# An attention and expert kernel: ranking steps moved and rewritten, and other products before the first real one

## The reference, cut to what matters

```python
x = x + xattn(layernorm(x), ctx, Wq, Wk, Wv, Wo, bo)     # x (4, 256, 128), ctx (4, 1601, 96)
x = x + ffn(layernorm(x), ...)                            # 1024 tokens

def xattn(x, context, Wq, Wk, Wv, Wo, bo):                # 8 heads of 64
    q, k, v = heads(x @ Wq), heads(context @ Wk), heads(context @ Wv)
    attn = softmax(q @ k.T * 64 ** -0.5)
    return merge(attn @ v) @ Wo + bo

def ffn(flat, router_w, router_b, sw1, sb1, sw2, sb2, rw1, rb1, rw2, rb2):   # 8 experts
    probs = softmax(flat @ router_w + router_b)
    top, idx = top_k(probs, 2)
    weights = zeros_like(probs).at[rows, idx].add(top)    # not normalised again
    shared = gelu(flat @ sw1 + sb1) @ sw2 + sb2
    h1 = gelu(einsum('td,edh->teh', flat, rw1) + rb1)
    return shared + einsum('ted,te->td', einsum('teh,ehd->ted', h1, rw2) + rb2, weights)
```

## Time and profile before

| | |
|---|---|
| median of 3 runs | 435.71 us |
| profiled execution: time, span | 435.49 us, 433.7 us |
| TensorE, products, busy | 420.8 us, 97% of the span |
| VectorE, ScalarE, GpSimd busy | 278.3, 219.3, 257.8 us |
| chain that ended last, by engine | TensorE 83%, GpSimd 8%, VectorE 3%, ScalarE 2% |
| mean granted clock of TensorE | 0.992 of full speed |

### The profile page before, as it was taken

The page is one execution under the profiler, slowest core; times in us unless marked ns, Lnnn a source line. Parts: engine busy times, 40 slices in busy tenths (PEclk is TensorE's granted clock), DMA queues, the critical chain, the costliest instruction groups (busy, mean ns, idle before and its releaser), DMA issues.

```text
span 433.7 us, 7166 instructions
## 1 busy us (share of the span) xinstructions
PE 420.8 (97%) x2500; PEld 327.0 (75%) x2500; DVE 278.3 (64%) x553; ACT 219.3 (51%) x384; POOL 257.8 (59%) x176
## 2 busy tenths in 40 slices
PE   8999999999999999999999999999999999878997
PEld 6787777786877877777878786778686776756896
DVE  4785858785546858673458596743495865656553
ACT  3555353342763534336735353447244754883783
POOL 4628995868474849382757483917352900873981
PEclk9999999999999999999999999999999999997999
DMA  7400002000000020000000300000000032003200
GB/s 227 139 1 2 0 2 59 0 2 0 2 0 2 2 58 2 0 2 0 2 2 0 110 2 2 2 1 0 2 2 2 2 97 79 19 1 112 85 26 24
DMA packets 16329, 11.59 MB, mean 27 GB/s; under 512 B 9580, under 2 KB 13208, under 8 KB 16296
## 3 DMA queue, kind: packets, MB, share of 16 engines
q1 hardware_dynamic: 16296, 11.15, 9.5%
HBM read 10.55 MB, written 0.56 MB: 26 GB/s over the span
## 4 chain that ended last, share of the span: by engine, by line
PE 83%; POOL 8%; DVE 3%; ACT 2%; issue 1%; DMA 1%; SPq 1%; POOLq 0%; ACTq 0%
PE ps L1254 19%; PE ps L1238 10%; PE ps L1174 10%; PE ps L1239 10%; PE ps L1240 10%; PE ps L1086 7%; PE ps L1088 7%; PE ps L1087 7%; POOL work L559 4%; PE ps L1128 2%; PE ps L1186 1%; POOL g_lo L773 1%; DMA probs<-in_L_xattn_Wv_dram 1%; POOL w_lo L757 1%; POOL work L557 1%
## 5 line engine op out<-in xcount | busy, mean ns | idle before, releaser
L849 ACT ACTIVATE probs<-ps 128x512 f32<-128x512 f32 (+1 forms) x208 | 123.8, 598 | 134.8 <-PE ps L1240 127.8
L970 DVE TENSOR_REDUCE maxes<-ps 128x1 f32<-128x402 f32 x256 | 131.6, 567 | 55.4 <-PE ps L1174 55.3
L559 POOL TENSOR_TENSOR work<-work,probs 128x1024 f32<-128x1024 f32 x54 | 128.9, 2388 | 15.9 <-ACT probs L849 13.0
L1254 PE MATMUL ps<-probs,v_sb 128*64 128x256 f32 (+1 forms) x832 | 93.4, 381 | 0.0
L1254 PEld LDWEIGHTS ps<-probs,v_sb 128*64 128x64 f32 (+1 forms) x832 | 58.3, 137 | 33.9 <-ACT probs L849 3.7
L1238 PE MATMUL ps<-g_hi,ctxT_hi 97*128 97x512 f32 (+1 forms) x208 | 82.9, 399 | 0.0
L557 POOL TENSOR_TENSOR work<-probs 128x1024 f32<-128x1024 f32 x14 | 33.5, 2392 | 82.0 <-issue 61.6
L1239 PE MATMUL ps<-g_lo,ctxT_hi 96*128 96x512 f32 (+1 forms) x208 | 82.0, 394 | 0.0
L1240 PE MATMUL ps<-g_hi,ctxT_lo 96*128 96x512 f32 (+1 forms) x208 | 81.7, 393 | 0.0
L1174 PE MATMUL ps<-ctxT_hi,g_hi 96*128 96x402 f32 x256 | 72.6, 356 | 0.7 <-ACT ctxT_hi L788 0.4
L773 POOL TENSOR_TENSOR g_lo<-probs,g_hi 128x512 fp32r<-128x512 f32 x32 | 40.5, 1290 | 35.1 <-ACT g_hi L871 35.1
(11 more groups left out here) (147 smaller groups left out, 526.4 us busy)
## 6 DMA issues: line engine op xcount, KB each, us to landing
v_sb<-weight_rows SPq DMA_DIRECT2D x12, 256.0 KB, 4.0
raw<-in_ctx_T_dram SPq DMA_DIRECT2D x3, 600.4 KB, 4.5
work<-in_L_ffn_rw_dram SPq DMA_DIRECT2D x1, 1024.0 KB, 7.5
raw<-weight_rows SPq DMA_DIRECT2D x4, 256.0 KB, 3.6
g_hi<-neg_row SPq DMA_DIRECT2D x60, 0.5 KB, 2.0
raw<-in_ctx_T_dram SPq DMA_DIRECT2D x3, 150.8 KB, 2.8
x_sb<-in_x_dram SPq DMA_DIRECT2D x1, 384.0 KB, 5.6
early<-in_WqkT_dram SPq DMA_DIRECT2D x1, 336.0 KB, 5.1
```

What stands on the lines that cost most here:

```text
L559: ops.tensor_tensor(acc, acc, pr, ALU.add).then_inc(summed, 1)
L849: nc.scalar.activation(probs[0:rows, n % SLOTS, j, :], s_bank(chunk_no(*w))[0:rows, :], ACT.Exp, scale=SCALE).then_inc(probs_ready, 1)
L970: v.tensor_reduce(maxes[:, p % 2, i * T + t, blk:blk + 1], src[:, 0:BW], AX.X, ALU.max).then_inc(ring_taken, 1)
L1254: ins = mm(o_bank[DH * i:DH * (i + 1), :], v_sb[0:rows, c, h * DH:(h + 1) * DH], probs[0:rows, n % SLOTS, j, i * S:(i + 1) * S], start=(c ...
```

## The change

- **Last half's routing.** The transposes of the last batch's rows (`xt`), the router and the exponential each move one turn later. `rank` comes at the end of turn 6 and the transposes of the weights at the end of turn 7, behind the second layer's products of that turn.
- **Ranking rewritten.** The two best are found from the logits less their maximum, not from the probabilities: `mark_best` replaces the two largest by 1.0 and makes a mask of them (`is_gt` 0.5). In the last half it follows the logits at once, beside the exponential. Then exponential times mask, sum, reciprocal, and one product written into all four groups of columns. In the last half the exponential and its masked form stand in PSUM. The low part of the weights is now made after the transposes (one more VectorE step). The first half uses the same steps on VectorE, GpSimd has none of them any more, and the first half's logits also have their maximum subtracted (one exponential instead of four).
- **w1 in three parts**: experts 0 to 2 after pair 0, 3 and 4 after pair 2, together with the addition of `bo`, 5 to 8 after pair 3.
- **Start.** Instead of 13 fp32 products of 128 rows and 64 columns: 8 pairs of `float32r` products, each of 64 rows, 128 stationary and 256 moving columns, on rows 0 to 63 and 64 to 127, into banks 4 and 5. The memset of `ones_r` stands ahead of that of `ones`. The later `keep_awake` calls stay.
- **First casts.** ScalarE converts all four blocks of the first context before `Wv`, and GpSimd takes two low parts before `wv_lo`.

```diff
-WARM = 13
+WARM = 8
...
-              (n_units + 1, 3): [("rank",), ("best",)], (3, 6): [("ring", ("wrow",))]}
+              (n_units + 1, 3): [("rank",)], (3, 6): [("ring", ("wrow",))]}
...
-        main += [("w1", k) for k in range(2) if n == 2 * k] + followers(n, n_units)
+        main += [("w1", k) for k, at in enumerate((0, 2, 3)) if n == at] + followers(n, n_units)
...
-    amid = {0: [("sums", last_pair), ("quotient", last_pair + (0,)), ("quotient", last_pair + (1,))], 2: [("ring", ("y", b))], 4: [("ring", ("xt", b))],
-            5: [("ring", ("router", last)), ("exp", last)], 6: [("rank", last), ("best", last)], 7: [("ring", ("wrow", last))]}
-    behind = {2: [("roots", b)], 3: [("norm", b)]}
+    amid = {0: [("sums", last_pair), ("quotient", last_pair + (0,)), ("quotient", last_pair + (1,))], 2: [("ring", ("y", b))], 5: [("ring", ("xt", b))],
+            6: [("ring", ("router", last)), ("exp", last)]}
+    behind = {2: [("roots", b)], 3: [("norm", b)], 6: [("rank", last)], 7: [("ring", ("wrow", last))]}
...
-    W1_CUT = NE - PAIRS
+    W1_PARTS = (slice(0, PAIRS - 1), slice(PAIRS - 1, PAIRS + 1), slice(PAIRS + 1, NE))
...
+        ones_r = sb("ones_r", [P, S], F32R)
...
+        lexp_bank, chosen_bank = (ps[:, O_BANK, i * TH * E:(i + 1) * TH * E].rearrange("p (t e) -> p t e", e=E)
+                                  for i in range(2))
+        def routing(w):
+            return (lexp_bank, chosen_bank) if w == NHALF - 1 else (lexp[:], chosen[:])
...
+            own(g.memset(ones_r[:].bitcast(F32), 1.0))
             own(g.memset(ones[:], 1.0))
...
             low_part(0, 0)
+            low_part(0, 1)
             pool.wait_ge(s_wv, 16)
...
-                if kind == "scores" and w == (0, 3, NU - 1, 0):
-                    added(0, 3)
+                if kind == "w1" and w == 1:
+                    added(0, 2)
                     pool.wait_ge(xn_ready, B - 1)
                     pool.wait_ge(s_bo, 16)
                     g.tensor_tensor(x_sb[:], x_sb[:], bo_sb[:].unsqueeze(1).to_broadcast([P, NT, D]), ALU.add
...
+                    nc.scalar.activation(routing(w)[0], logit[:, :, 0:E], ACT.Exp).then_inc(lexp_ready, 1)
...
-                if p == 0 and b < 2:
-                    dve.wait_ge(w1_split, b + 1)
+                if (b, p) in ((0, 0), (0, 2), (1, 0)):
+                    dve.wait_ge(w1_split, ((0, 0), (0, 2), (1, 0)).index((b, p)) + 1)
...
+            def mark_best(w):
+                dve.wait_ge(logit_ready, w + 1)
+                for t in range(TH):
+                    ins = v.max(top8[:, t, :], logit[:, t, 0:E])
+                then_own(ins)
+                then_own(v.memset(top8[:, :, TOP:8], 1.0))
+                for t in range(TH):
+                    ins = v.match_replace(low[:, t, 0:E + 8 - TOP], top8[:, t, :], logit[:, t, 0:E + 8 - TOP], 1.0)
+                then_own(ins)
+                then_own(v.tensor_scalar(mask[:], low[:, :, 0:E], 0.5, None, ALU.is_gt))
...
+                        then_own(v.tensor_reduce(neg_lmax[:], lg, AX.X, ALU.max, negate=True))
+                        v.tensor_tensor(lg, lg, neg_lmax[:].unsqueeze(2).to_broadcast([P, TH, E]), ALU.add
                                         ).then_inc(logit_ready, 1)
+                        if b == NHALF - 1:
+                            mark_best(b)
...
-                        v.tensor_copy(wT[:, b * HALF:(b + 1) * HALF], src).then_inc(ring_taken, 1)
+                        cols = slice(b * HALF, (b + 1) * HALF)
+                        then_own(v.tensor_copy(wT[:, cols], src))
+                        v.tensor_tensor(wT[WLO:WLO + E, cols], src[WLO:WLO + E, :], wT[WLO:WLO + E, cols].bitcast(F32),
+                                        ALU.subtract).then_inc(ring_taken, 1)
                 elif kind == "rank":
+                    le, ch = routing(w)
+                    if w < NHALF - 1:
+                        mark_best(w)
                     dve.wait_ge(lexp_ready, w + 1)
+                    v.tensor_tensor(ch, le, mask[:], ALU.mult)
+                    then_own(v.tensor_reduce(lsum[:], le, AX.X, ALU.add))
                     then_own(v.reciprocal(rsum[:], lsum[:]))
...
+                    wr = wrow[:, w * TH:(w + 1) * TH, :].rearrange("p t (a r) -> p t a r", r=WLO)[:, :, :, 0:E]
+                    v.tensor_tensor(wr, ch.unsqueeze(2).to_broadcast([P, TH, P // WLO, E]),
+                                    rsum[:].unsqueeze(2).unsqueeze(3).to_broadcast([P, TH, P // WLO, E]), ALU.mult
+                                    ).then_inc(w_ready, 1)
...
-            keep_awake(WARM)
+            for _ in range(WARM):
+                for r in range(2):
+                    rows = slice(DH * r, DH * r + DH)
+                    mm(ps[:, 4 + r, 0:S], ones_r[rows, 0:P], ones_r[rows, :], start=True, stop=True)
+            pe.wait_ge(pool_done, 2)
```

More of the change, by code:

```diff
@@ L380, in build @@
         w_rows = sb("w_rows", [P, NHALF, HALF])
-        logit = sb("logit", [P, TH, E])
+        logit = sb("logit", [P, TH, E + 8])
+        mask = sb("mask", [P, TH, E])
         neg_lmax = sb("neg_lmax", [P, TH])
@@ L385, in build @@
         rsum = sb("rsum", [P, TH])
-        rprob = sb("rprob", [P, TH, E + 8])
+        chosen = sb("chosen", [P, TH, E])
         top8 = sb("top8", [P, TH, 8])
@@ L506, in twice @@
             return rows.rearrange("p t (a r) -> p t a r", r=W3)
-        def high_weights(rows):
-            return (twice(rows)[:, :, :, 0:E], w_hi[:].bitcast(F32).unsqueeze(2).to_broadcast([P, TH, P // W3, E]))
         def activations(n):
@@ L605, in _ @@
             load_ctx(1)
-            sp.wait_ge(pool_done, 4)
+            sp.wait_ge(pool_done, 5)
             sp.dma_start(b2_rows[0:E], rb2).then_inc(s_b2, 16)
@@ L697, in _ @@
             g.tensor_tensor(wv_lo[:], wv_sb, wv_hi[:].bitcast(F32), ALU.subtract).then_inc(w_split, 1)
-            for i in range(1, BLOCKS):
+            for i in range(2, BLOCKS):
                 low_part(0, i)
@@ L701, in _ @@
             pool.wait_ge(consts_ready, 2)
[L702 removed]
+            g.memset(logit[:], 1.0).then_inc(consts_ready, 1)
             pool.wait_ge(s_rw, 32)
@@ L752, in _ @@
                 if kind == "w1":
-                    es = (slice(0, W1_CUT), slice(W1_CUT, NE))[w]
+                    es = W1_PARTS[w]
                     pool.wait_ge(s_w1, 32)
-                    added(0, 2 * w)
+                    added(0, (0, 2, 3)[w])
                     then_own(g.tensor_copy(w1_hi[:, es], w1_sb[:, es]))
@@ L804, in _ @@
                 high_part(0, i)
-                if i == 1:
-                    act.wait_ge(s_wv, 16)
-                    nc.scalar.copy(wv_hi[:], wv_sb).then_inc(wv_hi_ready, 1)
+            act.wait_ge(s_wv, 16)
+            nc.scalar.copy(wv_hi[:], wv_sb).then_inc(wv_hi_ready, 1)
             for kind, w in steps:
@@ L995, in _ @@
                             dve.wait_ge(s_rw, 32)
-                        v.tensor_tensor(logit[:], src[:, 0:TH * E].rearrange("p (t e) -> p t e", e=E),
+                        lg = logit[:, :, 0:E]
+                        if b == 0:
+                            dve.wait_ge(consts_ready, 3)
+                            dve.wait_ge(s_rw, 32)
+                        v.tensor_tensor(lg, src[:, 0:TH * E].rearrange("p (t e) -> p t e", e=E),
                                         rb_sb[:].unsqueeze(1).to_broadcast([P, TH, E]), ALU.add).then_inc(ring_taken, 1)
                         dve.wait_ge(*taken(w))
[L999 to L1004, removed]
+                        then_own(v.tensor_reduce(neg_lmax[:], lg, AX.X, ALU.max, negate=True))
+                        v.tensor_tensor(lg, lg, neg_lmax[:].unsqueeze(2).to_broadcast([P, TH, E]), ALU.add
                                         ).then_inc(logit_ready, 1)
+                        if b == NHALF - 1:
+                            mark_best(b)
                     elif w[0] == "back":
@@ L1025, in _ @@
-                    then_own(v.tensor_tensor(rprob[:, :, 0:E], lexp[:], rsum[:].unsqueeze(2).to_broadcast([P, TH, E]),
-                                             ALU.mult))
-                    for t in range(TH):
-                        ins = v.max(top8[:, t, :], rprob[:, t, 0:E])
-                    then_own(ins)
-                    then_own(v.memset(top8[:, :, TOP:8], -1.0))
-                    for t in range(TH):
-                        ins = v.match_replace(low[:, t, 0:E + 8 - TOP], top8[:, t, :], rprob[:, t, 0:E + 8 - TOP], 0.0)
@@ L1033, in _ @@
-                    ins.then_inc(ranked, 1)
-                elif kind == "best" and w == NHALF - 1:
-                    dve.wait_ge(ranked, w + 1)
-                    dve.wait_ge(wrow_zero, 2)
-                    wr = wrow[:, w * TH:(w + 1) * TH, :]
-                    weight = wr[:, :, W4:W4 + E]
-                    then_own(v.tensor_tensor(weight, rprob[:, :, 0:E], low[:, :, 0:E], ALU.subtract))
-                    then_own(v.tensor_copy(w_hi[:], weight))
```

(4 more changed lines are left out.)

7 lines of the change are left out of this document (1 added, 6 removed).

## The result

The changed kernel took 432.92 us, the median of 12 runs (431.64 to 435.31), against 435.7 us for 12 runs of the kernel before beside them: ratio 0.9933, 95% interval 0.9915 to 0.9951. So it is faster, by 2.8 us and not by the 6.9 us of the forecast, and 1.1 us outside the range. Its profiled execution is one of the long ones, 435.31 us (span 433.3), 2.4 us above the median; so it hardly differs from the profiled one of before, and is read here for places, not for the total.

The account below looks back on a forecast made before the run. TensorE, busy nearly all the span, was taken as the bound, so only its idle and slow time could go. 435.49 - 8.0 - 0.8 + 1.9 = 428.6, with the median 0.2 above: 428.8 us; range 425.6 to 431.8.

Parts of the forecast that it names:

- Part 1: Ranking of the last half, expert stage: TensorE's waits and low clock go, a new 0.7 us idle comes; 8.0 us gained.
- its own balance, 8.8 less 0.7: Last half's ranking: waits and low clock gone, together 8.8 us, less the new idle of 0.7 before the router.
- So no wait is left there, and no low clock: Transposes of the last half's routing weights: weights ready at 386.9 to 387.6, so TensorE doesn't wait there or slow down.
- Part 2: Ranking of the first half, near 255 us: subtracting the maximum stalls on GpSimd's addition; 1.9 us lost.
- TensorE stops at 256.1 for **1.9 us: First half: VectorE's stalled subtraction delays the maxima, so TensorE lacks a free ring bank; 1.9 us, not regained before attention ends.
- Part 3: w1 converted in thirds: GpSimd's additions end earlier and the wait before the first pair's row sums goes; 0.8 us gained.
- Part 4: Start: 26 instructions on 64 columns become 16 on 256, ending at 3.1 or 5.0 us; cost taken as 0.
- The path does not run there ... I take 0: Start: the first v product waits for GpSimd's split starting at 9.12, so the new warming products cost 0.
- Its bound of +1.9: Start: up to 1.9 us lost if TensorE were still at the low clock when the first v product starts at 10.5.
- the rival with +1.4: Start: the new products raise the clock later, 1.4 us lost, 430.2; chance 0.11. The same as rival (c).
- rival (c): Start: clock rises later because TensorE ends at 3.1 and idles until the weights arrive; +1.4, 430.2 us; chance 0.11.
- rival (e): Last half: the later router makes the ranking as late as now, so the 5 us idle stays; 434.5 us, chance 0.04.

Follow-up runs that it names:

- e5: Changed kernel with the old start (13 fp32 products of 64 columns) and the maximum subtracted with one operand in PSUM; 428.59 us, ratio 0.9847.
- e10: Same kernel as e9 (changed kernel, 11 fp32 products filling TensorE's wait near 257 us), run again for its profile; 430.61 us, ratio 0.9875.
- e1: Changed kernel with the start of before: 13 fp32 products of 128 rows and 64 columns, no pairs; 431.69 us, ratio 0.9911.
- after_again: The changed kernel, unaltered, measured once more for a second profiled execution; 433.07 us, ratio 0.9945.
- e6: e5 with three rounded 512-column products filling TensorE's wait before the last half's router; 427.15 us, ratio 0.9815.
- e2: Changed kernel with the logits left in PSUM until their maximum is subtracted, so one operand is in PSUM; 429.18 us, ratio 0.9851.
- e9: Changed kernel with 11 fp32 products of 64 columns put into TensorE's wait near 257 us; 430.2 us, ratio 0.9876, profiled execution disturbed.
- e4: Kernel before with only w1 in three parts and the output bias addition put behind the second; 435.02 us, ratio 0.9984.
- e3: Kernel before with only the new start (8 pairs of 64-row products in the rounded format); 436.87 us, ratio 1.0029.
- e8: Changed kernel with its 16 warming products all on the first 64 rows, so none overlap; 432.87 us, ratio 0.9935.
- e7: Changed kernel with 13 pairs of the new warming products instead of 8; 431.73 us, ratio 0.9906.
- e11: Changed kernel with its 16 warming products on all 128 rows, not in pairs; 431.82 us, ratio 0.9918.

## Why the prediction was wrong, by its own steps

**Direction and mechanism held, the size did not.** Put into the profiled executions by the runs: -0.8 for w1 (365.4 to 364.6 in e5), +1.8 for the start (12.27 - 10.50), +1.9 for the stall (e10 against e5), +3.1 for the low clock behind it (e1 against e10), which makes 6.0 where 5.9 us were measured at the first gelu; then -6.3 in the expert stage. The forecast had -0.8, 0, +1.9, nothing, and -8.0.

**Part 1.** The timetable came out: an idle of 0.55 us before the router (0.7 forecast), the mask stalled to the end of a GpSimd instruction (0.88 us instead of 0.18), weights at 393.3, which is 387.6 plus the 5.7 us by which the router was later than forecast, no wait at the transposes, nothing late in the tail. Where the clock stayed high the stage took 50.4 to 50.6 us (after_again, e6, e10) against 58.3, which is 7.7 to 7.9: the 8.0 was right for that case (its own balance, 8.8 less 0.7, makes 8.1). The step that failed is "So no wait is left there, and no low clock": the new idle was priced at its own length, and in seven of the nine profiles with it the clock fell behind it, for 1.5 us more.

**Part 2.** The stall is right in mechanism and size: the same kind of operation, 2.12 us instead of 0.19, TensorE stopped (1.59 us as the list of waits counts it), and attention ended 1.9 us later for it (e10 against e5). The Trainium skill's rule in "SBUF — State Buffer", section "Who interferes with whom", was weighed rightly. The runs agree with it from the other side too: with one operand in PSUM the stall is gone (e2, 0.19 us). The failed step is "TensorE stops at 256.1 for **1.9 us**" taken as the whole price. The earlier trace rows had shown what a wait does to the clock, and Part 1 even counts it as a gain (7 slots of 0.2, and the transposes) where a wait goes; I didn't charge it where a wait comes. It cost 2.5 us in the medians (e9, e10) and up to 3.1 in a profile, more than the stall. This is the largest missed term.

**Part 3.** Right in its place (e4's trace), and in size as far as it can be told.

**Part 4.** "The path does not run there ... I take 0" failed. The path did not run there at full clock; at half clock everything from 3.4 to 10.9 us is longer and the first v product is late by 1.8 us. Its bound of +1.9 and the rival with +1.4 were right: 1.3 us in the medians (e1, e3). That pairs overlap was right (2.07 us). The reason that rival (c) gave, the idle time before the weights, was not: e8 has none and is late, e10 has it and is early.

**The sum again.** Forecast 428.8; plus 1.3 (start), 2.5 (clock after the stall) and some 0.7 (half of the 1.4 by which e6 beats e5, for a dip that comes in some executions only; an estimate): 433.3, measured 432.9. This is an account and no test, since its terms are differences of the same medians. All three are one term, the clock behind a new idle or weak stretch. I had put it into one rival, on the start alone, with 0.11, as though the three were unrelated; so the range was too narrow on its upper side. The same term is missing in rival (e): with an idle of 5 us its low clock, 2.0 us in Part 1's own balance, would have stayed too, and 434.5 leaves it out. With the three mended, e6 took 427.15, where the sum without them and without the stall, 435.7 - 8.0 - 0.8, is 426.9.

What stays open: whether half the rows alone make the start's clock late; why the same wait brought a low stretch of 6.8 us in four profiles and of 3.4 us in two, and why the dip after the router, or the late rise with the same start, came in some executions and not in others.

## What to carry to other kernels

Price every new idle of TensorE twice: its length, and half of what may run at the low clock behind it, even for 0.6 us of idle; in the first half the second was the larger, 2.5 us against 1.9. An idle that can't be removed can be filled, with products written where they do no harm: that gave back 2.5 us (e9, e10), and in e6 1.4 us in the medians, which is not resolved, beside a clock that stayed high in all five runs. And a small VectorE step on a busy path should have an operand in PSUM while GpSimd works: 0.19 us against 2.12.

## What the runs showed of the hardware

- The clock fell while TensorE was busy again: the wait ended at 258.73, and the clock was low from 260.1 to 266.9, with products all through it. So the price stands behind the wait, where a list of waits shows nothing.
- In one profile each: behind products on 64 of the 128 rows, one at a time for 3.5 us, the clock stayed low until 11.0 us; with the same on 128 rows it rose at 4.2 us, and with pairs on both row groups for 3.2 us at 5.1 us.
- A pair of 64-row products on two row groups took about the time of one product, at the low clock: 26 products in 3.15 us (0.12 each, e7) against 16 on all rows in 3.53 us (e11) and 15 on one row group in 3.56 us (e8), 0.22 to 0.24 each.
- A 128x32 subtraction of VectorE with both inputs in SBUF took 2.12 us beside a GpSimd addition, 0.19 us without one, and 0.19 us beside it with one input in PSUM (e2).
